# Output norm in the scan stage: the row sums and squares made on ScalarE in place of VectorE's bn_stats

## The reference: what is computed

```python
def _layernorm(x, axis=-1, eps=1e-05):
    m = jnp.mean(x, axis=axis, keepdims=True)
    v = jnp.var(x, axis=axis, keepdims=True)
    return (x - m) / jnp.sqrt(v + eps)
...
h = jax.nn.relu(adj @ x @ gcn_w + gcn_b)
h = (h - mu) * lax.rsqrt(var + EPS) * ln_g + ln_b
# _mamba: xc, z = h @ w_in; u = silu(conv(xc)); dbc = u @ w_xp
dt = jax.nn.softplus(dbc[:, :DT_RANK] @ w_dt + b_dt)
dA = jnp.exp(dt[:, :, None] * A[None])
dBu = dt[:, :, None] * B[:, None, :] * u[:, :, None]
hst = dAt * hst + dBut            # scan over the rows, 16 states
y = (ys + u * D_skip) * silu(z) @ w_out
...
x = _layernorm(x + _L0_gnn_ref(...), axis=-1)
x = _layernorm(x + _L1_gnn_ref(x, adj, ...), axis=-1)     # the last line: the output norm
```

## Time and profile before

| what | value |
|---|---|
| median of 3 runs | 1144.08 us (1141.78 to 1144.95) |
| profiled execution, its own time | 1143.51 us |
| span from first to last instruction in it | 1141.6 us |
| VectorE busy | 1036.0 us, 91% |
| TensorE busy | 984.3 us, 86% |
| ScalarE busy | 527.2 us, 46% |
| GpSimd busy | 295.3 us, 26% |
| scan stage, windows 0 to 7 | about 540 to 1142 us |

### The profile page before, as it was taken

One profiled execution on the slowest core, in us unless ns is written; L12 is line 12 of the kernel. 1 busy time (PEld: TensorE's weight loads), 2 busy tenths in 40 slices (PEclk: granted clock), 3 DMA queues, 4 the chain that ended last, 5 costly groups with the idle time before them and its releaser, 6 DMA issues. The chain is left out here.

```text
span 1141.6 us, 13185 instructions
## 1 busy us (share of the span) xinstructions
PE 984.3 (86%) x4162; PEld 677.3 (59%) x4162; DVE 1036.0 (91%) x858; ACT 527.2 (46%) x946; POOL 295.3 (26%) x197
## 2 busy tenths in 40 slices
PE   0689999999999999999988979979889799685555
PEld 0567777777777877444555646646556465463444
DVE  1999999999999999724999999999999999999994
ACT  1343343434444342324555555736456556564431
POOL 5321112020202110102323224332333243322340
PEclk9999999999999999999999999999999999896776
DMA  9999999999999999847444253254441542101100
GB/s 263 225 178 304 332 330 347 322 349 326 326 355 321 352 329 310 189 180 257 159 158 166 94 203 133 72 207 146 164 182 61 202 147 75 38 20 55 38 9 10
DMA packets 190908, 226.37 MB, mean 198 GB/s; under 512 B 8624, under 2 KB 164336, under 8 KB 176528
## 3 DMA queue, kind: packets, MB, share of 16 engines
q1 hardware_dynamic: 105920, 163.60, 43.9%
q10 hardware_dynamic: 81856, 54.80, 18.8%
q0 software_dynamic: 3088, 7.47, 2.1%
HBM read 162.66 MB, written 63.18 MB: 198 GB/s over the span
## 5 line engine op out<-in xcount | busy, mean ns | idle before, releaser
L807 DVE STREAM_TRANSPOSE at<-rows 128x1024 f32<-128x1024 f32 x136 | 267.7, 2009 | 21.6 <-DMA rows<-in_adj 8.4
L507 POOL TENSOR_TENSOR dBuP<-dtu,b_sb 128x1024 f32<-128x1024 f32 x64 | 153.5, 2398 | 397.5 <-DVE hs L960 227.5
L1025 PE MATMUL yT<-ah,xh 128*128 128x512 f32 x512 | 211.1, 412 | 47.8 <-DVE al L815 42.7
L547 ACT ACTIVATE ah<-at 128x2048 fp32r<-128x2048 f32 x64 | 122.5, 1915 | 210.2 <-PE yT L1025 208.6
L1112 PE MATMUL bank<-adjc,xm 128*128 128x512 f32 x448 | 210.7, 599 | 1.6 <-ACT axT L625 1.6
L1025 PE MATMUL yT<-ah,xl 128*128 128x512 f32 x512 | 200.5, 392 | 0.0
L1025 PE MATMUL yT<-al,xh 128*128 128x512 f32 x512 | 200.5, 392 | 0.0
L1196 PE MATMUL yT<-ident,pr 128*128 128x128 f32 x1024 | 152.5, 299 | 38.0 <-DVE pr L967 38.0
L714 ACT ACTIVATE dA<-dt,A_sb 128x512 f32<-128x512 f32 x256 | 169.7, 713 | 26.2 <-DVE dt L914 26.0
L1196 PEld LDWEIGHTS yT<-ident,pr 128*128 128x128 f32 x1024 | 132.2, 154 | 65.0 <-DVE pr L967 51.4
L967 DVE TENSOR_TENSOR pr<-hs,bank 128x1024 f32<-128x1024 f32 x128 | 153.0, 1196 | 3.9 <-PE bank L1192 3.8
(11 more groups left out here) (150 smaller groups left out, 994.2 us busy)
## 6 DMA issues: line engine op xcount, KB each, us to landing
adjT<-at SPq DMA_DIRECT2D x56, 1024.0 KB, 7.8
adjc<-adjT SPq DMA_DIRECT2D x56, 1024.0 KB, 5.0
rows<-in_adj SPq DMA_DIRECT2D x152, 256.0 KB, 8.3
rows<-in_adj ACTq DMA_DIRECT2D x136, 256.0 KB, 8.8
b_sb<-b_dram ACTq DMA_DIRECT2D x32, 512.0 KB, 3.7
xm<-in_x SPq DMA_DIRECT2D x4, 512.0 KB, 16.2
xs<-in_L_gnn_x ACTq DMA_DIRECT2D x4, 512.0 KB, 17.1
res<-in_x POOLq DMA_DIRECT2D x8, 256.0 KB, 7.2
```

What stands on the lines that cost most here:

```text
L507: nc.gpsimd.tensor_tensor(dBu(n, par)[:, :, 1:], dtu[par][:, :, :], b_sb[pair % 2][:, nB(n) % 2:nB(n) % 2 + 1, :].to_broadcast([P, H, TILE ...
L547: nc.scalar.activation(ah[c % 2][:, :], at[c % 2][:, :, :].rearrange("p m t -> p (m t)"), ACT.Copy)\
L807: last = nc.vector.transpose(dst.rearrange("p m (g i) -> p g m i", i=32), src.rearrange("p g (i m) -> p g m i", i=32))
L1025: last = mm(acc[k][:, :], w[:, b, :], v[c % 2][:, cols], start=(b == 0 and j == 0), stop=(b == KB - 1 and j == 2))
```

## The change

VectorE's step 11 loses `tail_stats`. ScalarE gets a new `tail_stats` in step 12 of each window with a tail, behind the front's L671 and L672. It makes four passes (Identity, scaled by -1/128) over the 128 x 128 groups in PSUM whose accumulator output is minus the mean; after a wait for these, four passes of Square with minus the mean as bias, whose accumulator output is the sum of squared deviations; after another wait, one small instruction that gives variance plus epsilon. The full-size output of the eight passes goes to `o_n`, which `tail_norm` overwrites later. For that it waits that the last tile's `o_n` is stored. The statistics of the last tile, behind window 7, stay on VectorE, and so do those of the front's own norm (`front_g`).

```diff
-          ... dve_gate=1, dve_tail=11, pe_tr=3,
+          ... act_exp=13, act_ts=12, act_tail=14, ... dve_gate=1, pe_tr=3,
...
+                    if tail and n == AT['act_ts']:
+                        tail_stats(b - 1)
                     if tail and n == AT['act_tail']:
                         tail_norm(b - 1)
+
+            def tail_stats(b):
+                act.wait_ge(projected, b + 1)
+                wait(act, o_mean_scaled, b)
+                wait(act, out_stored, 16 * b)
+                for q in range(RG):
+                    nc.scalar.activation(o_n[:, q, :], O[:, q, :], ACT.Identity, scale=-1.0 / D, accum_out=mr2[:, q:q + 1])\
+                        .then_inc(o_mean, 1)
+                act.wait_ge(o_mean, RG * (b + 1))
+                for q in range(RG):
+                    nc.scalar.activation(o_n[:, q, :], O[:, q, :], ACT.Square, bias=mr2[:, q:q + 1],
+                                         accum_out=sq2[:, q:q + 1]).then_inc(o_squares, 1)
+                act.wait_ge(o_squares, RG * (b + 1))
+                nc.scalar.activation(ve2[:, :], sq2[:, :], ACT.Identity, scale=1.0 / D, bias=eps_ln[:, 0:1]).then_inc(o_var_eps, 1)
...
-                    if tail:
-                        if n == AT['dve_tail']:
-                            tail_stats(b - 1, 1 - par)
...
-            tail_stats(TILES - 1, 1)
+            tail_stats(TILES - 1)
```

More of the change, by code:

```diff
@@ L39 @@
 AT = dict(pool_rs=3, pool_tail_rs=13, dve_dt=14, act_hn=4, act_hT=5, act_silu=9, act_bc=11,
-          act_sp=12, act_exp=13, act_tail=14, dve_g=1, dve_bc=9, dve_sp=12, dve_gate=1, dve_tail=11, pe_tr=3,
+          act_sp=12, act_exp=13, act_ts=12, act_tail=14, dve_g=1, dve_bc=9, dve_sp=12, dve_gate=1, pe_tr=3,
           pe_z=7, pe_dbc=8, pe_dt=10, pe_turn=2, pe_out=9, act_b0=14, act_b1=2, act_b2=5, act_b3=9, act_ax=15, act_g=0, act_start=1, act_skip=2, act_y=4)
@@ L111, in gnn_mamba @@
         mr2 = sb("mr2", [P, RG])
+        sq2 = sb("sq2", [P, RG])
         nb2 = sb("nb2", [P, RG])
@@ L250, in gnn_mamba @@
         y_gated, projected = sem("y_gated"), sem("projected")
-        o_stats, o_mean_var, o_var_eps, o_inv_dev = sem("o_stats"), sem("o_mean_var"), sem("o_var_eps"), sem("o_inv_dev")
+        o_mean, o_squares, o_var_eps, o_inv_dev = sem("o_mean"), sem("o_squares"), sem("o_var_eps"), sem("o_inv_dev")
+        o_stats, o_mean_var = sem("o_stats"), sem("o_mean_var")
         o_mean_scaled, o_normed = sem("o_mean_scaled"), sem("o_normed")
@@ L923, in tail_gate, with tail_stats @@
                                         sz[par][:, :, :].rearrange("p q d -> p (q d)"), ALU.mult).then_inc(y_gated, 1)
-            def tail_stats(b, par):
+            def tail_stats(b):
                 dve.wait_ge(projected, b + 1)
@@ L929, in tail_stats @@
                 last.then_inc(o_stats, 1)
-                dve.wait_ge(o_stats, b + 1)
+                dve.wait_ge(o_stats, 1)
                 nc.vector.tensor_copy(stat_in[:, :], stats2[:, 0, 0:1])
@@ L934, in tail_stats @@
                 last.then_inc(o_mean_var, 1)
-                dve.wait_ge(o_mean_var, b + 1)
+                dve.wait_ge(o_mean_var, 1)
                 nc.vector.tensor_scalar(mr2[:, :], mv2[:, :, 0], -1.0, 0.0, ALU.mult, ALU.add)
```

## The result

The changed kernel takes 1141.62 us in the median of 22 runs (1139.16 to 1143.92), against 1143.3 us of the kernel before in 22 runs beside it. The ratio is 0.9984 (0.9976 to 0.9991): 1.8 us faster, between 1.0 and 2.7. That is inside the 0.3% that were called "the same", but on the other side of zero than the +2.3 us of the forecast. The profiled execution took 1139.99 us, its span is 1138.4 us.

A forecast was written before the change was run, and what follows sets the result against it. VectorE, busy 91% of the span, was taken to bound the kernel. Window moves of +5.2, -1.3 and -1.6 sum to +2.3 us on the profiled 1143.51, giving 1145.8 us, range 1138 to 1154.

The forecast's parts named there:

- the same: Forecast case for the whole time: within 0.3% (3.4 us) of no change, X between 2.7 and 4.0; chance 0.44.
- What is removed: VectorE's statistics ahead of dBu: 1.57 us in each of windows 1 to 7, at most 11.0 us gained.
- What else moves: Start of scan 12, POOL's norm pair, ScalarE's norm pass, store and PE: all put at no cost.
- What is added, without the accumulators: ScalarE, step 12: eight passes, a small instruction and two waits, 2.2 us per window.
- The read of an accumulator: ScalarE, step 12: each of 8 passes gives out its sum, taken as 0.20 us, from nothing to 0.37.
- X: Whole addition on ScalarE in step 12 per window: 3.8 us as taken, 2.2 at least, 5.2 at most.
- Where it lands: VectorE's L904 (now L922) waits for ScalarE's one-plus: 5 times some 2 to 3 us, once under 0.5.
- the room: Old start of VectorE's L904 less old end of ScalarE's one-plus: 2.51 us in window 2, up to 5.10 in window 6.
- Window 7: No front and no L904 there, so this window was to gain all of 1.57 us.
- The reads are nearly free: Rival on ScalarE's accumulator reads: 0.06 us or less each, X 2.7 or less, -3.4 us or lower; chance 0.18.
- The reads are dear: Rival on ScalarE's accumulator reads: above 0.22 us each, X above 4.0, up to +10.7 us, 1154.2; chance 0.30.
- TensorE's clock: Rival: PE's clock falls after waiting at L904, up to 3.3 us more in five windows, 1151 to 1162; chance 0.08.

The follow-up runs named there:

- Twice the squares: The change with ScalarE's four squaring passes made twice, behind one more wait; 1145.73 us, 1.0024 against the kernel before.
- the kept statistics: The change with VectorE's eleven statistics instructions kept in step 11 too, reading a constant weight, results unused; 1146.41 us, 1.0020 against the kernel before.
- the kernel with the late statistics: The change with ScalarE's statistics in step 13, behind the Ln, in place of step 12; 1138.24 us, 0.9952 against the kernel before.

## Why the prediction was wrong

- **What is removed** (1.57 us of VectorE in 7 windows): right for VectorE's own work, and a little too much for the window. Where nothing waits for PE, window 3 is 72.09 us with the statistics ahead of the dt product, against 73.54 us for the undisturbed window 4 before: 1.45 us. The 0.1 us that is missing is scan 11 (see "What else moves").
- **What is added, without the accumulators** (2.2 us): right, 2.21 us measured.
- **The read of an accumulator** (0.20 us, from nothing to 0.37): this is the term that was mis-sized, and it alone turns the sign. It costs 0.09 us. I took the length of the nearest small instruction (L707, 741.15, 0.20 us), though in that trace the next one starts 0.1 us after it (L714, 741.25); for the passes I had used the distance between starts, for the reads the length. The argument that a read can hardly overlap its pass was wrong in this: the row of the read starts 0.15 us after a pass that reads as 0.29 us long. With X of 2.93 the same sum gives 5 x 2.93 - 13.85 - 3.14 = -2.3 us, against the measured -1.8 (-1.0 to -2.7). That it comes so close is partly luck. By the sum the waits would be 8.7 us, and they are 7.5; in the traces the waits for C rows are 0.8 us less and the scans 1.2 us longer in all. Together that is -3.1 us, where windows 1 to 7 show -3.2.
- **Where it lands** (L922 waits for the one-plus by X less the room): right. The wait came there, 5 times, and none in window 6, where under 0.5 us was said. Twice the squares and the kept statistics moved the waits by what the sum says (8.0 and 1.3 us). In size they were 0.8 us in window 1 and 1.4 to 1.8 in windows 2 to 5, where X of 2.93 and the room of 2.51 give 2.0 in window 2. The room is a distance read from one trace, and was 2.51, 2.88 or 3.41 us in windows of that same trace; what sets it was not tested.
- **Window 7** gained 1.6 us, as said (65.99 to 64.37).
- **What else moves, at nothing**: not quite. ScalarE's norm pass did not wait in windows 1 to 6. But scan 11 was put at nothing, and it takes 2.45 to 2.53 us in every window of all kernels that have no statistics on VectorE, against 2.35 before and 2.34 or 2.35 where the statistics are kept. Without them dBu 12 follows at once, and scan 11 starts 0.3 us ahead of the end of POOL's dBu 13. This takes back 0.9 us of the 11.0. It was also wrong to leave POOL at "2.2 us of cover" without saying what a late piece there would collide with; the kernel with the statistics behind the Ln shows it, since there POOL's dBu 15 ran beside a scan and cost more than a wait.
- **Rivals.** "The reads are nearly free" (X of 2.7 or less) was nearer in the price than the forecast, with 0.09 us a read and its limit at 0.06, though X of 2.93 still lies in the forecast's own case (2.7 to 4.0). "The reads are dear" fell. So did TensorE's clock: in the stretch that matches 760 to 770 (758.4 to 768.4 now) the granted clock is 0.89, and was 0.83; VectorE's waits for C rows in windows 1 to 7 are 2.0 us, and were 2.8. The 3.3 us of the waits shown with the result contain 1.3 of window 0, which the change does not touch. In window 7 the granted clock is lower than before (0.60, 0.69), but VectorE waits for nothing there.
- **Two slips in the working** change nothing: `projected` comes 5.7 us, not 5.5, ahead of the end of the start of scan 12 (1096.04 and 1101.76), and five times 3 us on 1145.8 us is 1161, not 1162.

## What to carry to other kernels

Price an instruction that joins a queue of short ones by the distance between starts, not by its length, and use one and the same measure for all terms of a sum. Before work is moved to an engine with a low busy share, look at the place: here the move was worth 2 us with the nine instructions between the dt product and a hand-over that the full engine was waiting for, and 14 us with them ahead of the dt product, in a wait of ScalarE. When a helper engine comes late, look for what its next piece will then run beside.

## What the runs showed of the hardware

**A scan on VectorE and a multiplication on POOL get in each other's way.** In the kernel with the late statistics, scan 13 took 3.40 us in place of 2.44 while POOL's dBu, started 1.1 us earlier, ran beside it. The other way round, POOL's small `nb` instruction takes 2.24 us when it starts beside a scan, and 0.20 us when it does not. The one that starts first seems to keep the way. The Trainium skill (SBUF — State Buffer, Who interferes with whom) says that a VectorE instruction with two inputs in SBUF contends with a GpSimd instruction that reads SBUF, and that the order of issue decides which one blocks; the trace agrees, with 3.40 us against 2.44.

The same shows in small at scan 11. POOL's dBu 13, scan 11 and `nb`, first with the statistics ahead of the dt product (window 3), then dBu 13 and scan 11 of the kernel before (window 2):

```profile
802.59 2.38 POOL L509 TENSOR_TENSOR dBuP<-dtu,b_sb 128x1024 f32<-128x1024 f32 x1 [6.36 <-DVE hs L978]
804.67 2.46 DVE L978 TENSOR_TENSOR_SCAN hs<-dA,zero,dBuP 128x1026 f32<-128x1026 f32 x1
808.01 0.20 POOL L500 TENSOR_TENSOR nb<-mr,rs 128x4 f32<-128x4 f32 x1
```

```profile
732.87 2.38 POOL L507 TENSOR_TENSOR dBuP<-dtu,b_sb 128x1024 f32<-128x1024 f32 x1 [6.93 <-DVE hs L960]
736.52 2.35 DVE L960 TENSOR_TENSOR_SCAN hs<-dA,zero,dBuP 128x1026 f32<-128x1026 f32 x1
```

A scan that starts 0.30 us ahead of the end of POOL's dBu takes 0.11 us more, one that starts 1.25 us ahead of it 1.05 more, and in windows 1 to 7 of all eleven traces no scan that starts clear of it takes over 2.36 us. That makes the added time about 0.2 us less than the overlap.

**A low TensorE clock ahead of a window's gate goes with 1.1 us of VectorE's waits in that window, in windows 2 to 5.** Two stretches of 4 us ahead of a gate in the kernel before (length, busy and count of each engine, PEclk), and VectorE's waits for PE in the window that follows the first of them:

```profile
760.07:764.07 4.00, 3.64 (x14) 3.09 (x15) 3.71 (x4) 2.08 (x6) 1.71 (x1) 0.58 0.00 0
834.94:838.94 4.00, 3.64 (x18) 2.51 (x19) 3.71 (x4) 3.45 (x9) 1.65 (x1) 1.00 0.43 131
...
773.83 1.22 DVE L967 TENSOR_TENSOR pr<-hs,bank 128x1024 f32<-128x1024 f32 x1 [0.22 <-PE bank L1192]
790.33 1.22 DVE L967 TENSOR_TENSOR pr<-hs,bank 128x1024 f32<-128x1024 f32 x1 [0.46 <-PE bank L1192]
798.80 1.22 DVE L967 TENSOR_TENSOR pr<-hs,bank 128x1024 f32<-128x1024 f32 x1 [0.47 <-PE bank L1192]
```

At 0.58 in the stretch ahead of window 3, between the levels of 1.2 and 2.4 GHz, VectorE waits 0.22, 0.46 and 0.47 us for PE's C rows, 10 to 35 us behind the gate, and the window takes 74.87 us. With the clock at 1.00 ahead of window 4 there is no such wait, and it takes 73.54 us. In the other traces the same pair appears: clock of 0.57 to 0.60 and waits of 0.9 to 1.15 us, in 4 windows of the kernel that keeps both statistics, and in one to two of most others. Window 6, in which PE has no adjacency blocks, does not follow it: before the change it has 0.57 ahead of its gate, no wait, and 73.49 us. That the clock is the cause was argued from these pairs and not shown by an edit. How many windows have it differs between kernels, which makes differences of 1 to 4 us here that no term of the sum contains; which window has it differs between runs of one kernel (window 4 in one trace of the kernel with the statistics ahead of the dt product, window 3 in the other).

**The last stretch, from the last gate to the end, varies by 3 us with the clock.** In it PE turns and projects the last tile, and no other work hides it. The kernel before, the one ahead of the dt product in its two traces, and the one behind the Ln:

```profile
1125.92:1141.60 15.68, 5.67 (x32) 5.25 (x32) 2.79 (x12) 2.59 (x6) 1.21 (x2) 0.72 0.05 17
```

```profile
1114.91:1128.90 13.99, 4.04 (x32) 3.62 (x32) 2.79 (x12) 2.59 (x6) 1.21 (x2) 0.87 0.07 19
```

```profile
1113.88:1129.50 15.62, 5.67 (x32) 5.25 (x32) 2.80 (x12) 2.59 (x6) 1.21 (x2) 0.72 0.06 17
```

```profile
1119.44:1136.70 17.26, 7.35 (x32) 6.76 (x32) 2.80 (x12) 2.70 (x6) 1.21 (x2) 0.60 0.05 15
```

15.7 us at a granted clock of 0.72, 14.0 at 0.87, 17.3 at 0.60; PE's busy time goes from 4.0 to 7.4 us with the same 32 matmuls. So 1.7 us of what the first run of the kernel ahead of the dt product shows over the kernel before in its profiled execution come from here, and not from the moved statistics. They are chance: the second trace of the same kernel has 15.6 us, as most others do. In that trace the span is 12.1 us shorter than before, of which the seven windows have 11.1 and the time ahead of the first gate, which the change does not touch, has 1.0; the three other executions of the same run were 0.9 to 1.4 us faster still. So the gain from the moved statistics is 10.8 to 11.2 us of shorter windows in the traces of these kernels, and the 1.6 to 3.7 us by which the medians of the kernels without a wait at L922 and without a slowed scan 13 went beyond 11.0 stay open.
